# A warm-up activation that writes to a tile of its own: an AdaLN block with attention and eight experts on one core

## The reference

```
h = layernorm(x) * (1 + ca) + sa                # sa, ca, ga, sb, cb, gb from silu(c) @ wmod
q, k, v = split(h @ w_qkv)                      # 16 heads of 64
q, k = softmax(q * 64**-0.5, over channels), softmax(k, over tokens)
x = x + ga * (((q^T k) applied to v) @ w_out + b_out)
h = layernorm(x) * (1 + cb) + sb
gate_probs = softmax(h @ Wg + bg)               # 8 experts, the best 2 are kept and renormalised
e = gelu(h @ W1 + b1) @ W2 + b2                 # per expert, tanh form of gelu, hidden width 1024
x = x + gb * sum over experts of e * selected
```

## Time and profile before

| | us |
|---|---|
| median of 3 runs | 826.16 |
| lowest and highest | 825.31, 827.48 |
| the profiled execution, its own time | 826.16 |
| its span, from the first to the last instruction | 824.4 |

### The profile page before, as it was taken

How to read it: one execution, slowest core, us unless ns; L and a number is a source line. 1 busy time by engine, 2 the same in 40 slices (tenths; PEclk the granted TensorE clock), 3 DMA queues, 4 the chain that set the end, 5 groups by cost and what they waited for, 6 DMA issues and landing times.

```text
span 824.4 us, 16791 instructions
## 1 busy us (share of the span) xinstructions
PE 759.8 (92%) x5848; PEld 697.1 (85%) x5848; DVE 611.4 (74%) x1319; ACT 465.5 (56%) x845; POOL 339.9 (41%) x291
## 2 busy tenths in 40 slices
PE   5889999999999889974599999999999999999993
PEld 4767777888888668974499999999999999999993
DVE  6899999988899624779666767776676876876652
ACT  4464565665744432257465657474656665765461
POOL 2342323323322011400245555656556565656553
PEclk9999999999999999975599999999999999999997
DMA  7500000000000125560225353535335245232332
GB/s 273 169 1 1 1 2 2 1 2 1 1 2 1 52 103 174 178 203 4 91 81 111 93 115 51 157 51 157 50 57 151 54 90 117 46 53 53 58 53 39
DMA packets 45650, 59.71 MB, mean 72 GB/s; under 512 B 8018, under 2 KB 38804, under 8 KB 45460
## 3 DMA queue, kind: packets, MB, share of 16 engines
q0 software_dynamic: 14400, 21.98, 14.8%
q1 hardware_dynamic: 31188, 36.93, 13.8%
HBM read 40.63 MB, written 18.27 MB: 71 GB/s over the span
## 4 chain that ended last, share of the span: by engine, by line
PE 75%; DVE 17%; issue 4%; POOL 1%; ACT 1%; DMA 1%; DVEq 0%; SPq 0%; POOLq 0%; ACTq 0%
PE ps L1637 24%; PE ps L1651 23%; PE ps L1455 7%; PE ps L1413 6%; PE ps L1538 3%; PE ps L1476 3%; DVE at_hi L1210 3%; PE ps L1611 2%; DVE q_max L933 2%; PE ps L1464 2%; DVE q_sum L940 2%; DVE k_blk L1043 2%; PE ps L1558 1%; DVE q_exp L934 1%; DVE ln_s L897 1%
## 5 line engine op out<-in xcount | busy, mean ns | idle before, releaser
L846 ACT ACTIVATE hid<-ps,b_col 128x256 f32<-128x256 f32 (+1 forms) x232 | 106.1, 509 | 114.1 <-PE ps L1637 82.2
L1651 PE MATMUL ps<-w_hi,hid_hi 128*128 128x256 f32 x544 | 153.6, 282 | 0.0
L1651 PE MATMUL ps<-w_lo,hid_hi 128*128 128x256 f32 x544 | 151.3, 278 | 0.0
L1651 PE MATMUL ps<-w_hi,hid_lo 128*128 128x256 f32 x544 | 151.3, 278 | 0.0
L1334 DVE TENSOR_TENSOR hid_lo<-hid,hid_hi 128x512 fp32r<-128x512 f32 (+1 forms) x116 | 91.0, 784 | 75.3 <-ACT hid_hi L850 72.5
L1637 PE MATMUL ps<-xT_hi,w_hi 128*128 128x256 f32 (+1 forms) x464 | 140.5, 303 | 2.2 <-DVE xT_lo L1297 2.2
L1637 PE MATMUL ps<-xT_hi,w_lo 128*128 128x256 f32 (+1 forms) x464 | 140.3, 302 | 0.0
L1637 PE MATMUL ps<-xT_lo,w_hi 128*128 128x256 f32 (+1 forms) x464 | 140.3, 302 | 0.0
L608 POOL DMA_INDIRECT out<-y,y_id x68 | 117.4, 1726 | 40.1 <-POOL y_id L603 17.6
L534 POOL TENSOR_TENSOR q_n<-q_exp,q_rec 128x1024 f32<-128x1024 f32 x32 | 61.0, 1905 | 174.7 <-DVE q_rec L941 174.7
L596 POOL DMA_INDIRECT listed<-xrows,gid x87 | 95.7, 1100 | 42.3 <-POOL gid L592 24.6
(11 more groups left out here) (214 smaller groups left out, 1475.6 us busy)
## 6 DMA issues: line engine op xcount, KB each, us to landing
w_raw<-in_L_ffn_W SPq DMA_DIRECT2D x16, 1024.0 KB
x_all<-in_L_attn_x SPq DMA_DIRECT2D x8, 512.0 KB, 9.8
out<-x_all SPq DMA_DIRECT2D x8, 512.0 KB, 3.0
xrows<-x_all SPq DMA_DIRECT2D x8, 512.0 KB, 4.7
listed<-xrows,gid POOLq DMA_INDIRECT x87
out<-y,y_id POOLq DMA_INDIRECT x68
wqk_raw<-in_L_attn_w_qkv SPq DMA_DIRECT2D x2, 512.0 KB, 6.3
wqk_raw<-in_L_attn_w_qkv SPq DMA_DIRECT2D x1, 1024.0 KB, 10.5
```

The source lines that it names most:

```text
L846: ins = act.activation(hid[:, m, 0:T], src, ACT.Gelu_apprx_tanh, bias=b1_col[:, e, m:m + 1])
L1651: last = pe.matmul(ps[:, bank, 0:D], a, w_, start=m == 0 and st, stop=m == M - 1 and sp_)
```

## The change

A tile `warm` of one float32 per partition is added, and the warm-up gelu writes to it instead of to the first column of `silu_t`.

```diff
         plan = sb("plan", [P, 2 * E], I32)
         wide, narrow = plan[:, 0:E], plan[:, E:2 * E]
+        warm = sb("warm", [P, 1], F32)
         tick = sb("tick", [P, 1], F32)
         gid = sb("gid", [P, BI], I32)
...
             act.wait_ge(s_const, CONSTS)
-            act.activation(silu_t[:, 0:1], mean_w[:, 0:1], ACT.Gelu_apprx_tanh)
+            act.activation(warm[:, :], mean_w[:, 0:1], ACT.Gelu_apprx_tanh)
             act.wait_ge(s_counts, 1)
```

## The result

The changed kernel is slower by 0.7%, a small loss that stands clear of the spread of the runs.

The account below looks back on a forecast made before the run. PE was taken to bound the kernel, with 75% of the chain, in attention and experts, DVE carrying routing. 824.4 us of span plus 1.76 outside it plus four zero terms gave 826.2 us, range 823.9 to 828.5.

Parts of the forecast that it names:

- The instruction itself: Warm-up gelu on ACT in routing: 0.20 us before and after, 7.92 us idle behind it, 0 on the path.
- No dependency went: The gelu's overwrite of silu_t comes 390 us after its last reader; no wait existed to be saved: 0.
- rival 1: Faster: POOL and DVE collide less where POOL's scaling runs, L1044's stalls shrink; a third of 9.0 us gives 823.2; chance 0.05.
- The tiles that shift, the line on PE: Matmuls with operands shifted by 32 bytes: 379 ns on wmod_sb and on fold, difference 0 ns, so 0 us.
- The form of the bound: Cost of the 32-byte shift taken from similar rows whose operands start on a multiple of 64 or 32 past: 0 us.
- Rival 2: Slower: PE pays for new places in attention and experts, 1 ns on each matmul, 5.3 us, 831.5 us; chance 0.06.
- The clock (rival 3): First expert pass: PE's clock rises at another moment, up to 2.1 us either way, 824.1 to 828.3 us; chance 0.12.
- The transfers: DMA at the kernel's end: taken as 0, bounded at 0.2 us either side; the skill's rule would give 0.06 us later.
- The range: Whole kernel: 823.9 to 828.5 us, from the clock's 824.1 to 828.3 and the DMA bound of 0.2.
- bounds of DVE and POOL: Shifted tiles on these engines: at most 1.0 us for DVE and 0.7 us for POOL, to either side.

Follow-up runs that it names:

- pad_only: The changed kernel with the added tile kept but the warm-up gelu writing to silu_t as before: 831.96 us, ratio 1.0082 to the kernel before.
- warm_unshifted: The changed kernel with warm placed last among the routing tiles, so no other tile moves: 825.92 us, ratio 0.9994 to the kernel before.
- sweep_2: Kernel before plus 24 groups of 54 unused matmuls behind the last expert block, varying distance, columns and float32 kind; at 256 float32r columns 113.3 ns (64), 119.8 (96).
- the sweep: Kernel before plus 20 groups of 42 unused matmuls behind the last expert block, at varied operand distances; 113.3 to 121.0 ns per matmul.

## Why the prediction was wrong

- **The instruction itself: right.** 0.20 us, 7.92 us of idle time behind it, nothing on the path. `pad_only` and `warm_unshifted` show it directly: with the destination alone the time does not move.
- **No dependency went: right.** Up to the experts the two executions stay within 0.14 us of each other. L1045, the operation whose long instances rival 1 put down to POOL, kept its mean (579 ns before, 578 after), so rival 1 had no part.
- **The tiles that shift, the line on PE: wrong.** This is the step that failed. I priced PE's share at 0 from the earlier trace rows, two median durations of 379 ns. Both rows are plain float32 matmuls, and `sweep_2` shows that these don't react to the distance. The profile prints "128x256 f32" for both kinds. The step tells them apart: 1.73 us for eight records, 216 ns, in L1538, against 114 to 120 in the second product, and the duration too, 379 against 279. The row on which the price of the experts' matmuls rested was of another kind of instruction. The term that I put at 0 measured 6.0 us, 3.7 ns on each of the second product's 1602 matmuls on the chain. After the change the two rows read the same as before, as forecast, and this said nothing:

```profile
L1442 PE MATMUL ps<-wmod_sb,silu_b x8: 379/379/462, 29.6 to 31.2; 128*128 128x256 f32 x8
...
L1539 PE MATMUL ps<-fold,h_all x128: 379/379/483, 310.8 to 354.1; 128*128 128x256 f32 x128
```

- **The form of the bound: wrong as well.** I asked where one operand starts, modulo 64. What the runs show is that the place of the two operands to each other counts: plus 64 bytes is not back at the fast value, plus 256 nearly is, and the sweep has differences for 4 bytes. The front part already held the facts: the left tiles move, `hid` on the right does not, and the second product takes one operand from each side. The first product takes both from the left, its distance stayed 0, and its step stayed at 119.8 to 120.0 ns.
- **The trace of before held a warning.** One product of the same shape ran at 120.0 ns (L1637, 5.76 us for 48) and the other at 113.7 (L1651, 3.41 for 30), with PE saturated in both. Equal work at two rates is a reason to ask what sets the rate before calling it untouchable.
- **Rival 2 was the right one, with chance 0.06.** Its time, 831.5 us, is within 0.3 us of the profiled 831.79, but by luck: it took 1 ns on 5263 matmuls, where in fact those of the second product paid 3.7 ns each, 6.0 us, and the first product and attention nothing. Its remark that the 379 ns rows can't show an effect of operands in pairs was the true objection, and it deserved more than a twentieth.
- **The clock (rival 3): within its bounds, and small.** The first pass took 10.10 us instead of 10.45, within the 2.1 us allowed, on the fast side; over all runs it took 10.03 to 10.76.
- **The transfers: not decided.** From the start of the last scatter-add to the end of the span it takes 824.4 - 815.03 = 9.4 us before and 830.0 - 820.53 = 9.5 after. The 0.06 us that the prediction estimated by the rule of the Trainium skill (DMA: Bandwidth & Descriptors, How a descriptor splits into AXI transactions) can't be told from that, so no run here confirms or refutes it.
- **The range** took in the bounds of DVE and POOL, 1.7 us, whose durations hardly changed (L1335 kept its median of 693 ns; POOL's L534 had a mean of 1905 ns before and 1903 after), and none for PE, which carries 75% of the chain. The zero was taken from the one pair that looked best.

The Trainium skill (SBUF — State Buffer, A bandwidth-pool intuition that's wrong (but worth ruling out)) gives TensorE "2nd independent read port for LDWEIGHTS", from which one would expect that the load of a stationary operand and the stream of the moving one don't disturb each other. In these runs the time of a pair depends on where the two operands lie to each other, by up to 7.7 ns in 113 (113.3 to 121.0 in the sweep); where the expectation and the measurement differ, the measurement decides. That it is the load and the stream that collide is my reading: it fits that plain float32, whose matmuls are nearly four times as long, shows nothing, and that the loss doesn't grow with the columns, but no run separated the two reads.

## What to carry to other kernels

Adding even a four-byte tile moves every tile behind it, and where PE sets the time, back-to-back float32r matmuls of 256 columns can gain or lose some 6% of their time by the relative placement of their two operands (here 0.7% of the kernel): put helper tiles where nothing follows them, and when a time changes without a changed instruction, compare the time per matmul of each product with that of before. To price such a shift, compare rows of the same kind of matmul (float32r with float32r) by their spacing, not by their duration, and look at pairs of operands that come from regions that move differently.

## What the runs showed of the hardware that I had not expected

- Back-to-back float32r matmuls of 128 x 128 by 256 columns, each behind a weight load of its own, run at 113.3 to 121.0 ns in the sweep, depending on where the two operands lie to each other: fastest at a distance of 64 and 192 bytes modulo 256, about 120 at 0 and 96. Finer steps count as well: 116.9 ns at 48, 119.5 at 68 and 121.0 at 72.
- At distances 64 and 192 two values occur, near 113.5 and 117.8, in one and the same program, and at 160 there were 120.0 and 118.6; what chooses is open.
- The best distance depends on the columns: at 384, 64 (173.1 ns) beats 96 and 192 (both 176.7); at 512, 0 (226.7) beats 64 (228.9) and 96 (233.1); at 128 the pieces lie 0.9 ns apart.
- Plain float32 matmuls of 256 columns take 431.7 ns a piece at four distances, without any difference.
